# A short convolution of four channel chunks: three on TensorE and one on VectorE, in place of two and two

## The reference

```
h  = layernorm(x) * g + b, scaled and shifted by a condition      (layer 0: positions permuted)
xz = h @ W_in                      # 256 -> 2 x 512; halves xm and z
xm = silu(conv1d(xm, conv_w) + conv_b)   # causal, 4 taps, each of the 512 channels by itself
dtr, Bm, Cm = split(xm @ W_xp)     # 64 + 16 + 16
dt = softplus(dtr @ W_dt + b_dt)
scan over the 256 positions: hst = hst * exp(dt*A) + (dt*xm) * Bm;  y = sum(hst * Cm)
out = x + gate * (((y + xm * D) * silu(z)) @ W_out)
```

## Time and profile before

| | |
|---|---|
| profiled execution | 5402.86 us, of which its span 5401.1 us |
| busy: VectorE / TensorE / GpSimd / ScalarE | 4656.6 / 4461.0 / 4060.0 / 3281.6 us |
| granted TensorE clock, mean | 0.899 |
| VectorE, taps of the convolution (L1073) | 192 instructions, 139.2 us |
| TensorE, taps of the convolution (L902) | 512 records, 229.9 us |
| load of the diagonal matrices | 32 of 512 KB |

### The profile page before, as it was taken

One profiled execution on the slowest core, in us unless ns is written; L12 is line 12 of the kernel. 1 busy time (PEld: TensorE's weight loads), 2 busy tenths in 40 slices (PEclk: granted clock), 3 DMA queues, 4 the chain that ended last, 5 costly groups with the idle time before them and its releaser, 6 DMA issues.

```text
span 5401.1 us, 54840 instructions
## 1 busy us (share of the span) xinstructions
PE 4461.0 (83%) x16792; PEld 2437.3 (45%) x16792; DVE 4656.6 (86%) x4552; ACT 3281.6 (61%) x5574; POOL 4060.0 (75%) x2840
## 2 busy tenths in 40 slices
PE   3678888888888888888888888888888888888765
PEld 1244444444444544444454444445444444544433
DVE  2885898999989898999998899898999999997573
ACT  2564565666666666766666676666666666665352
POOL 1874787878878787887877788777778878786562
PEclk8788798999989999999998999999999999998777
DMA  4763666666766676776666677666666766665362
GB/s 148 240 217 128 206 236 210 231 226 236 252 212 232 217 235 224 243 247 215 234 216 219 226 244 245 221 225 220 223 228 230 251 217 233 222 237 182 121 210 69
DMA packets 355050, 1164.53 MB, mean 216 GB/s; under 512 B 39347, under 2 KB 79330, under 8 KB 354758
## 3 DMA queue, kind: packets, MB, share of 16 engines
q1 hardware_dynamic: 310598, 1106.42, 59.9%
q10 hardware_dynamic: 44160, 54.60, 3.3%
HBM read 1140.78 MB, written 20.10 MB: 215 GB/s over the span
## 4 chain that ended last, share of the span: by engine, by line
DVE 34%; PE 31%; issue 11%; DMA 9%; ACT 8%; POOL 7%; SPq 1%; ACTq 0%; DVEq 0%; POOLq 0%
DVE hw L1234 16%; DVE ps L1220 7%; PE ps L1121 6%; PE ps L1472 5%; PE ps L1499 4%; DMA bs<-bc_scratch 4%; POOL hw L1252 4%; PE ps L893 3%; PE ps L1334 3%; ACT pts L1567 3%; DVE mx L1592 2%; DMA cs<-bc_scratch 2%; ACT da L1170 2%; DMA xhat<-in_x 2%; PE ps L1515 2%
## 5 line engine op out<-in xcount | busy, mean ns | idle before, releaser
L1252 POOL TENSOR_TENSOR hw<-hw,cs 128x1024 f32<-128x1024 f32 x1024 | 2416.0, 2359 | 755.4 <-DVE hw L1234 639.8
L1234 DVE TENSOR_TENSOR_SCAN hw<-da,ps 128x1024 f32<-128x1024 f32 x1024 | 2334.2, 2280 | 36.5 <-PE ps L1121 14.9
L1170 ACT ACTIVATE da<-dt,a_neg 128x510 f32<-128x510 f32 x2048 | 1327.0, 711 | 266.3 <-DVE hw L1234 262.8
L1259 POOL TENSOR_TENSOR hw<-hw 128x512 f32<-128x512 f32 x1024 | 1299.4, 1269 | 69.5
L1220 DVE TENSOR_TENSOR ps<-ps,bs 128x1024 f32<-128x1024 f32 x1024 | 1256.5, 1227 | 99.0 <-DMA bs<-bc_scratch 55.5
L1121 PE MATMUL ps<-hw,ident 128*128 128x512 f32 x2048 | 1135.1, 664 | 127.5 <-POOL hw L1259 127.3
L1121 PEld LDWEIGHTS ps<-hw,ident 128*128 128x128 f32 x2048 | 405.3, 211 | 593.5 <-issue 325.5
L893 PE MATMUL ps<-hT,w_in 128*128 128x512 f32 x1024 | 544.2, 663 | 83.9 <-DVE dt L1081 63.2
L1567 ACT ACTIVATE pts<-ps 128x512 f32<-128x512 f32 x512 | 280.2, 593 | 400.5 <-PE ps L1499 400.5
L1592 DVE TENSOR_REDUCE mx<-ps 128x2 f32<-128x512 f32 x512 | 330.0, 683 | 166.0 <-PE ps L1472 165.7
L770 ACT ACT_TABLE_LOAD x321 | 411.8, 1283 | 28.7 <-DVE x_c L1782 23.3
(11 more groups left out here) (180 smaller groups left out, 5370.7 us busy)
## 6 DMA issues: line engine op xcount, KB each, us to landing
bs<-bc_scratch SPq DMA_DIRECT2D x1024, 512.0 KB, 4.7
cs<-bc_scratch SPq DMA_DIRECT2D x1024, 512.0 KB, 4.8
taps<-taps_scratch SPq DMA_DIRECT2D x32, 512.0 KB, 6.7
xhat<-in_x ACTq DMA_DIRECT2D x16, 512.0 KB, 6.3
gate<-gates_scratch ACTq DMA_DIRECT2D x64, 128.0 KB, 4.9
x_b<-in_x ACTq DMA_DIRECT2D x16, 512.0 KB, 9.0
x_scratch<-x_b ACTq DMA_DIRECT2D x16, 512.0 KB, 5.8
x_c<-x_scratch ACTq DMA_DIRECT2D x16, 512.0 KB, 5.9
```

The lines of the kernel that those rows point to most:

```text
L1170: ins = nc.scalar.activation(da[q % (AHEAD + 1)][:, k, :, 1:S], dt_[:, c, :].rearrange("p (b s) -> p b s", b=GB)[:, :, 1:S], ACT.Exp, scal ...
L1234: nc.vector.tensor_tensor_scan(tile[:, :, :].rearrange("p n t -> p (n t)"), da[s % (AHEAD + 1)][:, :, :, :].rearrange("p n b s -> p (n b s)"),
L1252: nc.gpsimd.tensor_tensor(tile[:, :, :], tile[:, :, :], cs[s % C_RING][:, :, :], ALU.mult)\
L1259: nc.gpsimd.tensor_tensor(tile[:, 0, :], tile[:, 0, :], tile[:, 1, :], ALU.add)\
```

## The change

Chunk 1 moves from VectorE to TensorE. Its pass on ScalarE becomes a copy, its silu one that reads the bank; `c1` takes the bank of m1, and `c2` takes the bank of `c0`, for which it now waits for `u0` and no longer for the last tap of chunk 1. The matrices in `taps` grow to three chunks. `PLACES` is replaced throughout; of its lines those of front0 in odd and front1 in even segments are shown.

```diff
-ON_PE = (0, 2)
+ON_PE = (0, 1, 2)
...
 def front_piece(sem, name):
-    pe = ["h0", "h1", "m0", "m1", "m2", "c0", "m3", "c2"]
+    pe = ["h0", "h1", "m0", "m1", "m2", "c0", "c1", "m3", "c2"]
...
-    dve = ["st", "mv"] + [f"cv{m}_{s}" for m in (1, 3) for s in (1, 2, 3)]
-    uses = [("h0", 0), ("h1", 1), ("m0", 2), ("m1", 0), ("c0", 1), ("m2", 2), ("m3", 2), ("c2", 0)]
+    dve = ["st", "mv"] + [f"cv3_{s}" for s in (1, 2, 3)]
+    uses = [("h0", 0), ("h1", 1), ("m0", 2), ("m1", 0), ("c0", 1), ("m2", 2), ("c1", 0), ("m3", 2), ("c2", 1)]
...
     "even": {
...
         "front1": {
-            "pe": [20.467, 20.633, 20.967, 21.133, 21.8, 25.9, 26.2, 26.82, 31.8],
-            "act": [18.6, 19.5, 19.7, 19.9, 20.767, 20.933, 25.6, 26.35, 26.475, 26.85, 28.3],
-            "dve": [19.732, 19.866, 23.665, 25.665, 26.553, 26.777, 27.165, 27.553, 27.777],
+            "pe": [20.7, 20.9, 22.443, 22.586, 22.729, 23.014, 25.9, 26.2, 27.5, 28],
+            "act": [19.725, 19.975, 20.35, 20.85, 21.6, 21.85, 23.86, 26.386, 26.529, 26.814, 27.6],
+            "dve": [19.732, 19.866, 27.665, 28.11, 28.22, 31.997],
...
         "lin_a": {
-            "pe": [18.1, 19.8, 20.8, 23.633, 23.967, 24.633, 24.967, 25.6, 26.66, 26.98, 27.14],
+            "pe": [19.633, 19.967, 21.1, 22.871, 23.157, 23.8, 24.8, 25.6, 27.4, 27.6, 27.7],
...
     "odd": {
         "attn_a": {
...
-            "dve": [5.832, 5.916, 11.027, 11.055, 11.082, 11.11, 11.165, 11.248, 11.275, 11.303, 11.397, 11.464,
-                   11.531, 11.598, 11.665, 11.732, 11.799, 11.866, 11.933, 12.11, 18.066, 18.132, 18.198,
-                   18.264, 20.665, 22.066],
+            "dve": [5.832, 5.916, 11.165, 11.372, 11.414, 11.498, 11.539, 11.581, 11.665, 11.707, 11.749,
+                   11.791, 11.832, 11.874, 11.916, 11.958, 12.082, 12.165, 12.248, 12.665, 18.066, 18.132,
+                   18.198, 18.264, 20.665, 20.832],
...
         "front0": {
-            "pe": [23.633, 23.967, 24.8, 25.54, 25.78, 26.02, 27.7, 27.9, 29.175],
-            "act": [20.3, 22.6, 23.65, 23.8, 23.95, 25.267, 25.433, 27.5, 27.7, 27.9, 29.85],
-            "dve": [22.132, 22.198, 26.665, 27.165, 27.665, 28.665, 28.832, 29.165, 31.83],
+            "pe": [23.633, 23.967, 24.55, 24.8, 25.05, 25.78, 26.02, 26.26, 27.8, 28.443],
+            "act": [19.5, 20.767, 22.433, 22.767, 24.243, 24.814, 24.957, 27.35, 27.6, 27.85, 28.35],
+            "dve": [21.553, 21.777, 28.082, 28.165, 28.665, 31.83],
...
         "lin_b": {
-            "pe": [12.6, 13, 14.189, 19.633, 19.967, 20.633, 20.967, 22.8, 26.26, 27.5, 28.1],
+            "pe": [12.755, 13.027, 15.8, 19.633, 19.967, 20.8, 21.8, 22.8, 25.54, 26.767, 27.033],
...
         "mid0": {
-            "pe": [28.425, 28.55, 28.675, 28.8, 28.925, 29.05],
+            "pe": [28.586, 28.729, 28.871, 29.014, 29.157, 30.8],
...
             pe.wait_ge(taps_in[l], 16 * g + 16)
             convolve(pc, 0)
             yield
+            pe.wait_ge(pc.of("xc1"), pc.upto(g, "xc1"))
+            convolve(pc, 1)
+            yield
             pe.wait_ge(pc.of("xc2"), pc.upto(g, "xc2"))
             project_in(l, pc, 3)
             yield
-            pe.wait_ge(pc.of("cv1_3"), pc.upto(g, "cv1_3"))
+            pe.wait_ge(pc.of("u0"), pc.upto(g, "u0"))
             convolve(pc, 2)
             yield
...
             copy_chunk(0)
             yield
-            tap(1)
+            copy_chunk(1)
             yield
...
             silu_u(0)
-            silu_sum(1)
+            silu_u(1)
             yield
...
-            for m in (1, 3):
+            for m in (3,):
```

More of the change, by code:

```diff
@@ L201 @@
         "front0": {
[L202 to L205, removed]
+            "pe": [8.8, 13.633, 13.967, 18.767, 20.633, 20.967, 23.8, 25.9, 27.633, 27.967],
+            "act": [2.35, 8.35, 8.85, 14.6, 17.6, 20.6, 21.6, 28.3, 28.5, 28.7, 29.6],
+            "dve": [4.11, 4.22, 29.553, 29.777, 30.11, 30.665],
+            "pool": [7.3, 27.3],
             "sp": [-1.28, -1.04],
@@ L208 @@
         "rest0": {
[L209 to L212, removed]
+            "pe": [-50, 2.767, 3.033, 4.633, 4.967, 7.8, 17.9, 19.033],
+            "act": [0.433, 0.767, 2.6, 2.85, 4.433, 4.767, 8.6, 16.6, 28.9],
+            "dve": [2.165, 10.665, 19.665, 30.22],
+            "pool": [2.8, 12.3, 20.8, 22.3],
             "sp": [-1.76, -1.52],
@@ L217 @@
         "attn_a": {
[3 rows of a table removed]
[L221 to L227, removed]
[3 rows of a table added]
+            "act": [2.386, 2.529, 2.814, 5.35, 5.6, 7.7, 7.9, 8.6, 10.433, 10.767, 11.267, 11.433, 11.6, 11.767,
+                   11.933, 12.35, 12.6, 12.85, 13.6, 14.6, 15.567, 15.633, 15.7, 15.767, 15.833, 15.9, 15.967,
+                   16.033, 17.6, 19.433, 19.767],
+            "dve": [1.165, 1.248, 8.464, 8.598, 8.866, 9.041, 9.082, 9.124, 9.165, 9.206, 9.289, 9.553, 9.777,
+                   10.082, 10.165, 10.248, 10.498, 10.665, 10.832, 11.665, 18.055, 18.11, 18.165, 18.22,
+                   21.165, 21.497],
+            "pool": [2.3, 18.3, 19.217],
             "sp": [-1.723, -1.631],
@@ L230 @@
         "attn_b": {
[4 rows of a table removed]
[L235 to L241, removed]
[4 rows of a table added]
+            "act": [22.433, 22.767, 23.7, 23.9, 25.6, 26.767, 27.143, 27.187, 27.23, 27.274, 27.317, 27.361,
+                   27.404, 27.448, 27.491, 27.535, 27.578, 27.622, 27.665, 27.709, 27.752, 27.796, 27.839,
+                   27.883, 27.926, 27.97, 28.013, 28.057, 28.171, 28.243, 28.314],
+            "dve": [21.665, 21.832, 28.018, 28.037, 28.055, 28.073, 28.092, 28.11, 28.128, 28.147, 28.165,
+                   28.183, 28.202, 28.22, 28.238, 28.257, 28.275, 28.293, 28.312, 28.665, 29.464, 29.598,
+                   29.732, 29.866, 30.041, 30.082],
+            "pool": [21.8, 27.8, 29.8],
             "sp": [-1.538, -1.446],
@@ L244 @@
         "back0": {
[L245 to L248, removed]
+            "pe": [-77.778, -55.556, -44.444, -33.333, 2.82],
+            "act": [-100.75, -100.375, -100.25, -100.125],
+            "dve": [-34.667, 0.11, 0.165, 0.22, 0.275],
+            "pool": [0.263, 0.525],
             "sp": [-1.908, -1.815],
@@ L251 @@
         "front1": {
[L252 to L255, removed]
+            "pe": [29.213, 29.257, 29.371, 29.443, 29.514, 29.586, 29.657, 29.729, 29.8, 29.871],
+            "act": [28.386, 28.457, 28.529, 28.6, 28.671, 28.743, 28.814, 28.886, 28.957, 29.029, 29.267],
+            "dve": [30.124, 30.165, 30.206, 30.247, 30.289, 30.665],
+            "pool": [30.675, 30.8],
             "sp": [-1.354, -1.262],
@@ L258 @@
         "mid0": {
[L259 to L262, removed]
+            "pe": [-100.8, -100.6, -100.4, -100.2, -88.889, -66.667],
+            "act": [-100.875, -100.625, -100.5, 0.025],
+            "dve": [-67.333, 0.055],
+            "pool": [0.788, 2.8],
             "sp": [-1.169, -1.077],
@@ L265 @@
         "mid1": {
[L266 to L269, removed]
+            "pe": [29.943, 30.014, 30.086, 30.157, 30.229, 30.8],
+            "act": [29.433, 29.6, 29.767, 29.933],
+            "dve": [30.497, 30.832],
+            "pool": [30.925, 31.3],
             "sp": [31.533, 31.867],
@@ L294 @@
         "back1": {
-            "pe": [11.586, 14.411, 17.9],
-            "act": [11.6, 15.62],
-            "dve": [13.777, 14.165, 15.665, 16.165, 16.497],
-            "pool": [12.883, 15.8],
+            "pe": [11.5, 14.411, 17.6],
+            "act": [12.85, 19.225],
+            "dve": [13.665, 14.165, 15.665, 16.165, 16.553],
+            "pool": [17.217, 17.383],
             "sp": [-0.689, -0.578],
@@ L440 @@
         "back1": {
[L441 to L444, removed]
+            "pe": [-85.714, -71.429, -57.143],
+            "act": [-87.5, -75],
+            "dve": [-67.333, -34.667, -1.6, -1.2, -0.8],
+            "pool": [-100.667, -100.333],
             "sp": [-1.891, -1.782],
```

189 lines of the change are left out of this document (96 added, 93 removed), and 35 rows, old and new, of the table PLACES.

## The result

The changed kernel takes 5548.07 us (median of four runs, 5538.51 to 5551.79), the kernel before beside it 5419.95: a ratio of 1.0243, 95% interval 1.0206 to 1.028. I had forecast 5461 and a range to 5510: the direction was right, the size was more than two times too small, and the time lies outside the range. The sum of +58 us stood on the profiled execution; from the one profiled execution to the other it is +142.4, by the medians +128.

A forecast was written before the change was run, and what follows sets the result against it. It took TensorE's full odd tails, followed by a fixed-latency chain, as the bound there, and VectorE as fuller in even tails. Terms 42 + 17 + 9 + 4 - 14 = +58 us on the profiled 5402.86 gave 5461, range 5375 to 5510.

The forecast's parts named there:

- (a): VectorE, every front: three instructions fewer, 2.2 us a front, 69.6 us over 32 fronts.
- (b): TensorE, odd tails: one chunk more, 3.4 us a front, taken as +3.0 a segment, +42 us over 14.
- (c): TensorE, even tails: the same 3.4 us against 2.2 us of idle, taken as +1.2 a segment, +17 us over 14.
- (d): TensorE, tails: chunk 2's new wait for ScalarE's u0 is covered, barely: 0, bounds 0 and +1.3 us.
- (e): Prologue: later projection, more diagonal blocks and larger tap writes, all exposed: +9 us, bounds +6 and +12.
- (f): Three fronts in the two double segments and the first: +1.2 us each, +4 in all, bounds 0 and +10.
- (g): Boundaries: the taps load, grown from 512 to 768 KB behind the first bs slice, costs 0, bounds 0 to +27 us.
- (h): ScalarE: as many passes as before, five table switches fewer in the first segment: 0, bounds -6 and 0 us.
- (i): Remaining new places: -14 us for row maxima in odd segments, 0 for all other reordering, bounds -20 and +20.
- the burst: Odd segments: attention's 16 row maxima run 1 before scan 11 and 15 behind, not 8 and 8: -1 a segment, -14 us.
- 1: Rival, all tails: VectorE is the real bound and TensorE's tail slides, so faster: 5328 at best, 5358; chance 0.18.
- Rival 3: Boundaries and tails: waits of (d) and (g) both come true, clock variant included, much slower: 5506; chance 0.13.

The follow-up runs named there:

- e4: Kernel before with VectorE's three instructions (taps) of chunk 1 left out, nothing else changed; ratio 0.9972.
- e3: Kernel before with chunk 0's four matmuls issued twice on TensorE, nothing else changed; ratio 1.017.
- e5: Kernel before at its own places, with chunk 0's matmuls issued twice and VectorE's taps of chunk 1 left out; ratio 1.0191.
- e2: Code of the kernel before at the changed kernel's new places, VectorE's taps of chunk 1 where they were; ratio 1.0239.
- e16: Changed code at the old places with m3 ahead of c1, run side by side with e17; ratio to the kernel before 1.0173.
- e17: Changed code at old places, m3 ahead of c1, and c1 behind the skip term in even segments; e13 run again, ratio to the kernel before 1.0138.
- e13: Changed code at old places, m3 ahead of c1, and c1 behind the skip term in even segments, first run; ratio to the kernel before 1.019.
- e6: Kernel before with one added wait: TensorE waits for ScalarE's u0 before chunk 2's convolution; ratio 1.0132.
- e1: Changed code at the places of the kernel before, chunk 1's matmuls right behind chunk 0's; ratio to the kernel before 1.0311.
- e14: Changed kernel with only ScalarE's hc0 and hc1 of the odd segments back at their old places; ratio to the kernel before 1.0301.
- e15: Kernel before with only one of chunk 0's four taps on TensorE, the other three left out, nothing moved; ratio 0.9978.
- e11: Kernel before with attn_a, lin_b, rest1 and back0 of the odd segments at the changed kernel's places; ratio 1.0162.
- e12: Kernel before with only the attention's first half (attn_a) of the odd segments at the changed kernel's places; ratio 1.0048.

## Why the prediction was wrong, step by step

- **(a)** right. VectorE's relief is worth 0 to 0.55% (e4), though it is the fuller engine by its busy share.
- **(b)** right as a price at the old places, 2.3 (e3) and 2.9 us (e5) an odd segment for the +3.0 that I took, and the tail windows of the changed kernel are 3.4 us longer. But at the new places it isn't an addition: e2 without c1 and the changed kernel with it, less VectorE's three taps, have odd segments of the same length, where at the old places the added work and the omitted taps together (e5) made them 2.9 us longer.
- **(c)** mis-sized at the old places: 3.2 to 3.4 us an even segment where I put 1.2, so some 30 us more. I counted the idle time of TensorE in the tail (2.2 us) as room. It wasn't: what hung on TensorE there was the skip term, which frees chunk 3 of u. Moving c1 behind it gave 21 us back (e16, e17), about two thirds of those 30. What the rest waits for is lin's out, by the profiles of e13 and e17 alone. The changed kernel's +3.0 an even segment has another source: step 26 is 1.2 us shorter there, and e2 has +4.0 without c1. It belongs to (i).
- **(d)** failed as a bound. "Covered, barely: 0" holds with the new places (15.6 us in 19 waits), but where it isn't covered TensorE waits 2.4 us a tail (75.2 / 31) and its clock falls besides, +71 us in all (e6), against my upper bound of 1.3 us a tail. I had the 2.75 us of ScalarE's chain in hand and took only half of them as exposed. In the timed kernel this cost doesn't stand.
- **(e)** 11.7 for 9. **(f)** 12 for 4, a little over its bound: the second segment alone took 16.2 us more and the first 4.8 less, of which the old code at the new places (e2) has 12.0 and 3.2, so most of it is order too. **(g)** The 0 isn't contradicted by e5 + e6 against e1, a test too coarse for its bound of 27 us; **(h)** 0 was not tested by itself.
- **(i)** failed, and it is the step that carries the miss: -14 for the burst, and "for all other reordering 0, bounds -20 and +20". The burst's half was right in its direction: steps 11 and 12 together gained 3.6 us a segment in the changed kernel, where I took 1. It is the 0 for the rest that was wrong, and I gave no reason for it but "mostly the same order". All the new places on the old code cost +129 us (e2), the gain of the burst included, as much as the whole change. On the new code they were worth 37 us less than the old places with c1 put in badly (e1), and 57 us more than those with c1 and m3 put better (e17).

So the sum erred twice: it put the reordering at next to nothing, and it added the prices of (b) and (c), some 59 us, to it, which at the new places did not come on top. That it got the direction right owes something to luck: it forecast slower for the added work on TensorE, and the steps that grew in the timed kernel are those of the reordering.

Of the rivals, 1 (VectorE is the bound) is refuted by e4 and e3. Rival 3 had the right mechanism in the wrong place: u0's wait and the lower clock behind it are real, but the new places keep them out of all but the prologue of the kernel that was timed; its other wait, for bs, did not come (61.0 us against 51.6).

My theory at the first runs was A, TensorE's added time sets the tail, against B, the new places cost it. A holds at the old places for more work (e3, e5), and what it expected of the stall at step 24 came (e14). It doesn't hold for less: e15 expected 50 to 85 us by it and 12 came. Nor does it explain the timed kernel, since e2 is as slow without the work. What the runs show is this: at the old places a piece added to TensorE came nearly by its full length (2.3 to 3.4 us of 3.4), and a piece taken away gave some 0.4 us of 2.6. That TensorE and VectorE are level in the tails (350.24 and 343.60 us busy of 353.40), so that each uncovers the other, would explain it and fits the new wait in e15, but it was not tested by itself. The Trainium skill ("Perfetto Trace Analysis", Identifying the Most-Contended Engine) says to take the engine of the highest occupancy and to optimize it first. Here that engine was VectorE with 86%, and 70 us of its work gone gave 15 (e4); the measurement decides.

Open: why the new places cost what they do, and so why the changed kernel is 1.0% slower than e17, which computes the same. By the segments of the two profiles it is 3.3 us in each odd one, 1.1 in each even one, 6 in the prologue and 11 in the second segment. Two candidates, the stall at step 24 and front0's early places, were tried in the changed kernel and moving them back didn't help. Not tried by themselves: the losses at steps 15 and 18 of odd segments (+1.7 and +0.9, the same in e2 and e11; +0.2 and +0.5 in e12), and the new places of the even segments, which no part run covers.
